# Moving an expert's output bias from a matmul on TensorE to VectorE, in a decoder layer with eight experts

## The reference

```
logits = silu(t @ rw1 + rb1) @ rw2 + rb2
vals, idx = top_k(logits, 2)
w = softmax(logits masked to those 2)
eh = silu(t @ ew1[e] + eb1[e])          # 512 hidden units, expert e
eo = eh @ ew2[e] + eb2[e]               # 256 outputs
y = t + sum over e of w[e] * eo[e]
```

## Time and profile before

| | |
|---|---|
| median of 3 runs | 492.98 us (492.39 to 494.41) |
| profiled execution | 493.77 us, span 491.9 us |
| TensorE busy | 457.1 us, 93% of the span |
| VectorE busy | 352.0 us, 72% |
| ScalarE busy | 280.2 us, 57% |
| GpSimd busy | 175.9 us, 36% |
| DMA | 54.37 MB, mean 111 GB/s |
| mean granted clock of TensorE | 0.979 |

### The profile page before, as it was taken

How to read it: one execution, slowest core, us unless ns; L and a number is a source line. 1 busy time by engine, 2 the same in 40 slices (tenths; PEclk the granted TensorE clock), 3 DMA queues, 4 the chain that set the end, 5 groups by cost and what they waited for, 6 DMA issues and landing times.

```text
span 491.9 us, 11187 instructions
## 1 busy us (share of the span) xinstructions
PE 457.1 (93%) x3670; PEld 323.7 (66%) x3670; DVE 352.0 (72%) x837; ACT 280.2 (57%) x715; POOL 175.9 (36%) x184
## 2 busy tenths in 40 slices
PE   5999989999999999999999999989799999999960
PEld 2456469856458966556895646778676787888840
DVE  5754667796866778686678688898668885555476
ACT  4273756626547535555761665563666777877830
POOL 1230124040204313012504020234346877777541
PEclk9799999999999999999999999999999999999995
DMA  8901000034230031621003424608113247223655
GB/s 324 376 13 45 0 2 0 29 103 160 98 129 0 0 128 43 213 85 44 1 0 128 122 92 131 246 16 350 47 45 122 79 135 268 78 81 84 195 197 213
DMA packets 20410, 54.37 MB, mean 111 GB/s; under 512 B 3365, under 2 KB 9774, under 8 KB 19600
## 3 DMA queue, kind: packets, MB, share of 16 engines
q1 hardware_dynamic: 16336, 43.32, 24.7%
q0 software_dynamic: 3744, 9.47, 6.7%
q10 hardware_dynamic: 288, 1.05, 0.6%
HBM read 36.98 MB, written 17.76 MB: 111 GB/s over the span
## 4 chain that ended last, share of the span: by engine, by line
PE 45%; issue 25%; DVE 14%; POOL 8%; DMA 5%; DVEq 1%; POOLq 0%; ACT 0%; ACTq 0%; SPq 0%
PE pj L1469 16%; PE op L1702 7%; PE pj L1683 4%; DMA picked<-wch,dst_row 3%; PE sc L1658 2%; POOL pn L461 2%; POOL picked L490 2%; DMA cst<-rows,src_row 2%; PE pj L1795 2%; POOL rstd L430 1%; PE sc L1556 1%; DVE stats L769 1%; POOL cst L479 1%; PE ov L1469 1%; PE tpA L1805 1%
## 5 line engine op out<-in xcount | busy, mean ns | idle before, releaser
L1469 PE MATMUL pj<-up,up_f 128*128 128x512 f16 x480 | 109.6, 383 | 2.8 <-DVE down L1313 1.1
L1469 PEld LDWEIGHTS pj<-up,up_f 128*128 128x128 f16 x480 | 46.3, 99 | 59.5 <-DVE rope L939 4.6
L679 ACT ACTIVATE p<-sc,nm 128x128 f32<-128x128 f32 x128 | 45.4, 369 | 38.3 <-DVE nm L1308 38.1
L461 POOL TENSOR_TENSOR pn<-p,inv 128x256 f32<-128x256 f32 x64 | 37.9, 614 | 79.3 <-DVE inv L1261 79.3
L479 POOL DMA_INDIRECT cst<-rows,src_row x39 | 48.7, 1248 | 19.9 <-issue 7.6
L490 POOL DMA_INDIRECT picked<-wch,dst_row x39 | 41.5, 1064 | 26.4 <-DVE wch L1252 9.9
L430 POOL TENSOR_TENSOR rstd<-veps,nhalf 128x4 f32<-128x4 f32 (+1 forms) x13 | 12.7, 975 | 103.2 <-DVE veps L777 102.9
L551 ACT ACTIVATE down<-pj,bias 128x512 f32<-128x512 f32 x48 | 32.6, 686 | 26.5 <-PE pj L1469 26.3
L1469 PE MATMUL pj<-up_f,up 128*128 128x512 f16 x192 | 43.4, 379 | 0.0
L1702 PE MATMUL op<-wch,outs 128*128 128x256 f16 x240 | 40.2, 273 | 0.0
L1683 PE MATMUL pj<-pT,v 128*128 128x128 f32 x256 | 34.3, 279 | 1.3 <-DVE outs L1279 0.8
(11 more groups left out here) (265 smaller groups left out, 1025.5 us busy)
## 6 DMA issues: line engine op xcount, KB each, us to landing
raws<-in_staged SPq DMA_DIRECT2D x12, 512.0 KB, 5.4
split<-halved SPq DMA_DIRECT2D x12, 512.0 KB, 3.2
down<-split SPq DMA_DIRECT2D x4, 1024.0 KB, 8.6
rows<-row SPq DMA_DIRECT2D x4, 528.0 KB
small<-in_x SPq DMA_DIRECT2D x4, 512.0 KB, 3.6
up<-in_ctx SPq DMA_DIRECT2D x4, 512.0 KB, 4.8
v<-in_w SPq DMA_DIRECT2D x2, 1024.0 KB, 9.2
resid<-outs SPq DMA_DIRECT2D x4, 512.0 KB
```

The lines of the kernel that those rows point to most:

```text
L461: pool.tensor_tensor(pn2[:, n % 2, k], p2[:, n % 2, k], inv2[:, n % 2, k].unsqueeze(2).to_broadcast([P, 2, P]), ALU.mult)\
L679: last = act.activation(p2[:, s, i, :], sc[s][:, i * P:(i + 1) * P], ACT.Exp, bias=nm2[:, s, i:i + 1], scale=1.0, accum_out=sum2[:, s, i:i ...
L1469: last = pe.matmul(out, w(c), v(c), start=(i == 0), stop=(i == len(terms) - 1))
```

## The change

The bias is loaded as float32 and broadcast to all 128 partitions once, 8 x 256 values in each, into the room of two attention buffers that are free by then. `weigh_out` gets it as the second input of its first operation, at the offset of the tile's expert, and needs three operations instead of two: PSUM low columns times `MID_DOWN` plus bias; PSUM high columns times `MID_DOWN` plus that; the sum times the gate. The gate value is now copied unscaled. The bias matmul, its table, the two halves and the DMA between partitions go. The three attention buffers `p2`, `pn2`, `pT2` become views of one tile `turns`, so that the bias can lie in the first two; its load waits until the last block was transposed.

```diff
+        turns = sb("turns", [P, 3 * 2 * 4 * P])
+        p2, pn2, pT2 = (turns[:, 1024 * i:1024 * i + 1024].rearrange("p (s h t) -> p s h t", s=2, h=4) for i in range(3))
+        b2 = turns[:, 0:E * D]
-        p2, pn2, pT2 = (sb(n, [P, 2, 4, P]) for n in ("p2", "pn2", "pT2"))
...
             sp.dma_start(b1, eb1).then_inc(small_in, 16)
-            sp.dma_start(b2f, eb2).then_inc(small_in, 16)
-            sp.dma_start(pick, pick_expert).then_inc(small_in, 16)
...
-            sp.wait_ge(b2_lo, 1)
-            sp.dma_start(b2[E:2 * E, :], b2l[0:E, :]).then_inc(b2_lo_in, 16)
+            sp.wait_ge(blocks_turned, 4 * G)
+            sp.dma_start(b2, eb2.rearrange("(a n) -> a n", a=1).broadcast_to([P, E * D])).then_inc(b2_in, 16)
...
-                        act.wait_ge(small_in, 48)
-                        copy(b2, b2f, UP).then_inc(b2_hi, 1)
+                        act.wait_ge(small_in, 16)
...
-                dve.tensor_scalar(gate[t % GATES][:], got[s].bitcast(F32)[:, bass.ds(e + D, 1)], MID_DOWN, None,
-                                  ALU.mult).then_inc(gated, 1)
+                dve.tensor_copy(gate[t % GATES][:], got[s].bitcast(F32)[:, bass.ds(e + D, 1)]).then_inc(gated, 1)
+                taken.append(e)
...
-                dve.tensor_scalar(ys[s], y[:, 0:D], g[:], None, ALU.mult).then_inc(y_part, 1)
+                if t == 0:
+                    dve.wait_ge(b2_in, 16)
+                dve.scalar_tensor_tensor(out=ys[s], in0=y[:, 0:D], scalar=MID_DOWN, in1=b2[:, bass.ds(taken[t] * D, D)],
+                                         op0=ALU.mult, op1=ALU.add).then_inc(y_part, 1)
                 dve.wait_ge(y_part, t + 1)
-                dve.scalar_tensor_tensor(out=ys[s], in0=y[:, D:2 * D], scalar=g[:], in1=ys[s],
-                                         op0=ALU.mult, op1=ALU.add).then_inc(y_free, 1)
+                dve.scalar_tensor_tensor(out=ys[s], in0=y[:, D:2 * D], scalar=MID_DOWN, in1=ys[s],
+                                         op0=ALU.mult, op1=ALU.add).then_inc(y_sum, 1)
+                dve.wait_ge(y_sum, t + 1)
+                dve.tensor_scalar(ys[s], ys[s], g[:], None, ALU.mult).then_inc(y_free, 1)
...
-                    dve.wait_ge(b2_hi, 1)
-                    dve.scalar_tensor_tensor(out=b2l[0:E, :], in0=b2f[0:E, :], scalar=UP, in1=b2[0:E, :], op0=ALU.mult,
-                                             op1=ALU.subtract).then_inc(b2_lo, 1)
...
-                pe.matmul(y[:, 0:D], pick[:, bass.ds(e * P, P)], b2, start=False, stop=True,
-                          skip_group_check=True).then_inc(y_full, 1)
...
-                    pe.wait_ge(b2_lo_in, 16)
```

More of the change, by code:

```diff
@@ L103, in decoder @@
                        "late"))
-    eb1, eb2, pick_expert = (a[k] for k in ("eb1", "eb2", "pick_expert"))
+    eb1, eb2 = a["eb1"], a["eb2"]
     rows = nc.dram_tensor("rows", [B * L, ROW // 2], U32, kind="Internal").ap()
@@ L262, in decoder @@
         room = Room(halved[:].bitcast(F32))
-        b1, b2f, b2, b2l = room.cells(E * MC), room.cells(D), room.cells(D, F16), room.cells(D, F16)
-        pick = room.cells(E * P, F16)
+        b1 = room.cells(E * MC)
         hot_t = room.cells((JO + JN) * REST)
@@ L289, in decoder @@
         RANK_NEW, TABLE_NEW = USE + 8, USE + 9
-        small_in, b2_hi, b2_lo, b2_lo_in = (sem(n) for n in ("small_in", "b2_hi", "b2_lo", "b2_lo_in"))
+        small_in, b2_in, y_sum = (sem(n) for n in ("small_in", "b2_in", "y_sum"))
         chain, counted, hot_t_done, pay_done, lanes_done = (
@@ L1230, in hidden_low @@
                                          op1=ALU.subtract).then_inc(h_lo, 1)
+            taken = []
             def take(t):
@@ L1806, in second_layer @@
                               start=(m == 0), stop=False, skip_group_check=True)
-                    pe.matmul(y[:, 0:D], hTl[q][:, m, :], down_rows[:, bass.ds(at, D)],
-                              start=False, stop=False, skip_group_check=True)
+                    last = pe.matmul(y[:, 0:D], hTl[q][:, m, :], down_rows[:, bass.ds(at, D)],
+                                     start=False, stop=(m == MC - 1), skip_group_check=True)
+                    if m == MC - 1:
+                        last.then_inc(y_full, 1)
                     if then is not None:
                         addresses(then, m)
-                pe.matmul(y[:, 0:D], pick[:, bass.ds(e * P, P)], b2, start=False, stop=True,
-                          skip_group_check=True).then_inc(y_full, 1)
             pe.wait_ge(sc_free[0], SC[0] * (G - 1) + 5)
@@ L1875, in extra_data @@
     data["eb1"] = n["L0_ffn_eb1"].reshape(E, MC, P).transpose(2, 0, 1).reshape(P, E * MC)
-    data["pick_expert"] = np.repeat(np.tile(16.0 * np.eye(E), (2, 1)), P, axis=1).astype(np.float16)
-    data["pick_expert"] = np.concatenate([data["pick_expert"], np.zeros((P - 2 * E, E * P), np.float16)])
-    data["eb2"] = np.concatenate([n["L0_ffn_eb2"], np.zeros((P - E, D), n["L0_ffn_eb2"].dtype)])
+    data["eb2"] = n["L0_ffn_eb2"].reshape(E * D)
     data["disp"] = np.concatenate([
```

## The result

The changed kernel takes 495.5 us (median of 18 runs, 494.06 to 497.19), the kernel before 492.43 (18 runs, 490.46 to 494.41): ratio 1.006, 95% interval 1.0048 to 1.0071. It is slower by 0.6%, 3.07 us. The prediction's range holds it; its likeliest case, +1.11 us and no measurable change, is too small by 2 us, and it is a slower case that came, at the lower edge of the first rival's 495.5 to 499.

The account below looks back on a forecast made before the run. It took VectorE, then TensorE, then DMA waits to bound the expert stage. Sum: -0.45 + 4.03 - 1.84 - 1.87 + 0.31 + 0.93 = +1.11 us on the median 492.98, so 494.1; range 490.5 to 499.0.

Parts of the forecast that it names:

- likeliest case: Whole kernel: +1.11 us to 494.1 us, 492.1 to 495.3 counted as no measurable change; chance 0.50.
- first rival: VectorE's new third operation stretched to 0.60 us, or address arithmetic exposed for 0.1 to 0.2: 497.3 us; chance 0.22.
- What bounds each stretch: Expert stage: VectorE full from 362.68 to about 404 us, then TensorE paces to about 459, then DMA waits rule.
- The three operations: VectorE's output step per tile: two constant forms at 0.41 us each plus handoffs of 0.04, the gate multiplication at 0.41.
- the addition of 0.31 us per tile: VectorE's output step grows from 1.00 to 1.31 us; over 13 steps of its full stretch 4.03 us are added.
- The sentence that costs the arithmetic of the bias's address at nothing: Output step: address arithmetic hidden by VectorE's hidden-layer work (0.68 us) in the full stretch, later by 0.87 us idle.
- The cover: VectorE's lead over TensorE's second layer of tile 14, 1.84 us, absorbs part of the addition; tile 14 starts 1.74 later.
- The refund: Tiles 14 to 30, paced by TensorE: the missing matmul gives back 17 x 0.11 = 1.87 us; tiles 1 to 13 don't count.
- VectorE has room after all: Rival: addition of 0.10 us or less stays within the cover, tiles 9 to 13 gain 0.11 each: 490.5 us; chance 0.17.
- The front's 0.45: Before the first tiles: removed VectorE subtraction saves 0.34 us (lower bound nothing), tile 0's missing matmul 0.11.
- The tail's +0.93: Last stretch: three additions of 0.31 us lie in line between waits for scatters; the last tile's is covered.
- GpSimd as the pacer: Rival: VectorE's third operation delays the scatter as well as the gather, 3.33 us per tile: 502.3 us; chance 0.11.

Follow-up runs that it names:

- late: Tiles 0 to 13 keep the bias matmul of the kernel before, tiles 14 to 38 get the bias by VectorE as in the changed kernel: 491.43 us.
- early: Tiles 0 to 13 get the bias by VectorE as in the changed kernel, tiles 14 to 38 by the matmul: 498.3 us.
- fixed_bias: Changed kernel, but the first output operation always reads the first expert's bias at a constant offset, without register arithmetic for the address: 494.35 us.
- no_bias: Kernel before without the bias matmul and with nothing in its place; all that prepares the bias stays: 489.43 us.
- no_gate: Changed kernel without the third output operation, so outputs are not multiplied by the gate value: 488.6 us.
- tucked_late: Bias by matmul for tiles 0 to 13, by VectorE for 14 to 38; VectorE's expert-number register load moved behind the hidden layer's low half: 490.81 us.

## Why the prediction came out as it did

- **What bounds each stretch** was right: late and early show it by themselves, 4.9 us lost before tile 14, 1.8 gained after.
- **The three operations** were priced a little too high in sum: 0.42, 0.42 and 0.35 us for 0.41, 0.41 and 0.41. The estimate of 0.30 us for the third was worked out from the Trainium skill, "VectorE: DVE Perf Modes", section "The perf-mode tier table"; the trace's 0.354 (median of 39) lies between that and the normalization's row. By durations alone the addition would have been even smaller.
- **The failed step** is the addition of 0.31 us per tile. I subtracted ends of operations from ends; the next work hangs on the *start* of the last output operation and on the register load behind it (408.46 for an operation that starts at 408.45), which the prediction nowhere counts. The sentence that costs the arithmetic of the bias's address at nothing is off too, by about 0.05. The addition is 0.39 in the paced part. In the full stretch the 13 steps cost 409.88 - 403.77 = 6.11 us plus the lead of 0.67 that VectorE had at the logits (362.01 after, 362.68 before): 6.78, or 0.52 each, against 4.03 forecast. Of that 13 x 0.39 = 5.07; two register loads that ran long (0.703 and 0.841 us; idle times of 0.87 and 1.00 instead of 0.47) make 0.93, where the longest before was 0.447 in that stretch; one more gap, 0.70 at 406.26, has a load of ordinary length: VectorE's queue stands 0.40 us at the semaphore wait behind it, against 0.05 at the others in that stretch, and what it waits for there I can't name. Of the rest, about 0.5, 0.22 lies between the gate copies and the next output steps, where the bias's address is worked out (0.057 us on VectorE's queue each time; fixed_bias has 0.56 less there); what remains within the steps is not settled. The two long loads are no accident of one execution: early and fixed_bias, whose steps there are the same, have them at the same two tiles. In each the third operation has moved the load from about 0.42 to about 0.82 us after the issue of a store (last section).
- **The cover** of 1.84 us was right in kind: 1.71 of it were used. 6.11 - 1.71 = 4.40 is what tile 14 is late, forecast 1.74.
- **The refund** was right: 1.71 for 1.87, period 2.86 for 2.85. That tiles 1 to 13 wouldn't count was not: no_bias gains 0.75 us there, 0.51 of it from tile 9 to 14, about 0.1 for each tile, as the rival "VectorE has room after all" had it for tiles 9 to 13.
- **The front's 0.45** is not what was seen. The traces differ by 0.71 us at the last block transposition already (336.30 to 335.59), and by as much, 0.72, on SyncE's queue at 296.79 (296.07 after), before anything of the change runs: the first load that the change takes away was issued at 311.64. The removed subtraction adds some 0.3 to that at first, but at the logits only 0.67 is left: ScalarE's activation at 357.30 waits 0.29 us for TensorE there, which it did not before, so there TensorE's work ends last. The lower bound, nothing, was the better value.
- **The tail's +0.93** fits the 1.25 between after and no_gate, but over all kernels that part runs from 31.92 to 34.35 us with no order that I can give: early and before end on two operations and have 33.33 and 34.35. The longest of all is before's profiled execution, which hides the loss in the pair of profiles. To tile 31 the change costs 358.43 + 52.26 + 49.55 - (358.98 + 47.31 + 51.26) = 2.69 us, which would leave 0.4 of the 3.07 for the tail, if both executions stand for their medians up to there.
- **The sum** was partly luck. At tile 31 the change is 2.69 us behind, where the forecast had -0.13 at tile 30; that the time came out only 2 us above the forecast would then be owed to a tail that added some 0.4 instead of the forecast's 1.24, and that the range held it is owed to the 8.5 us it spans.
- **The rivals.** What came is the size that I gave to the first rival (from 0.39 us per tile on), by another mechanism than a stretched operation or an exposed address of 0.1 to 0.2 us (fixed_bias: about 0.05): waits between instructions. GpSimd as the pacer is refuted (gather 1.03, scatter 1.00, idle 0.52). The Trainium skill, "SBUF — State Buffer", section "SBUF: two separate sides", says that a VectorE operation with two SBUF inputs shuts out, until it ends, a GpSimd operation that reads SBUF; the trace agrees in so far as the gather, which now begins ahead of that operation (429.00 against 429.40), is down from 1.36 to 1.03. That it is the gather's reading which waited no run shows. The load is hidden, as forecast.

## What to carry to other kernels

Price an operation added to an engine that works through its list in order by the distance from start to start, up to the next instruction that does the work others wait for, and read the engine's own register and wait instructions in that gap: they are not in the busy time. Here the register load cost nothing behind an operation of 0.68 us and 0.46 us behind one of 0.19, so its place can be worth more than the operation that is disputed. And before moving work to an engine because it is idle on average, look for the stretch in which it is full; an engine with slack in that stretch (here ScalarE) can take the piece that has no deadline.

## What was unexpected of the hardware

- The register load of one number from SBUF takes 0.30 us on VectorE's queue, with 0.19 and 0.02 us of register work behind it; the longest were 0.841 us in the changed kernel and 1.333 in tucked_late, for the same read of one number. The two long ones in the changed kernel (371.8 and 408.5) follow within 1 us on the issue of a store on SyncE's queue (370.97, 407.64); those are stores of `row` and `outs` from SBUF to DRAM. The other traces agree: over all fourteen, the 12 loads that began 0.81 to 1.43 us after the issue of one of these two stores took 0.69 to 1.33 us, and the 16 that began between 0.21 ahead of it and 0.66 after it took 0.30 to 0.37. That the store's DMA is the cause was not tried.
- An operation whose input is the engine's own last output waits for that by semaphore and follows 0.455 us after the start of one of 0.42; an independent one follows 0.27 us after the start of one of 0.35 (378.85 to 379.12), before its end.
